# Routed expert tiles on one core: the down product moved ahead of the up product in TensorE's order

## The chip, the core and the metric

The kernel runs on one core of a Trainium2 chip. TensorE (PE in the views) multiplies matrices, VectorE (DVE), ScalarE (ACT) and GpSimd (POOL) work on elements, and SyncE (SP) issues DMAs. Each engine takes its own instructions in the order in which the program lists them, and they meet at semaphores. Matmuls read on-chip memory and write PSUM, which has 8 banks here, `ps[:, bank, :]`. The metric is device time in microseconds (us), lower is better.

## What is computed

Six sublayers on x of 8 sequences of 512 tokens with 256 features. Two of the six, the first and the third, are a mixture of experts, and the change lies in them:

```python
def _L0_ffn_ref(x, w12, w3, shared_w1, shared_w2, shared_w3, router_w, expert_bias):
    ...
    shared = silu(xf @ shared_w1.T) * (xf @ shared_w2.T) @ shared_w3.T
    scores = sigmoid(xf @ router_w.T)
    _, top_idx = top_k(scores + expert_bias, 2)
    gates = scores * one_hot(top_idx, 8).sum(axis=-2)
    h1, h2 = split(einsum('td,ehd->teh', xf, w12), 2)
    h = silu(h1) * h2 * gates[:, :, None]          # 8 experts, 256 hidden
    return shared + einsum('teh,edh->td', h, w3)

x = x + 0.5 * _L0_ffn_ref(_layernorm(x), ...)      # sublayer 1: changed code
x = x + _L0_attn_ref(_layernorm(x), ...)           # gated linear attention
x = x + 0.5 * _L0_ffn_ref(_layernorm(x), ...)      # sublayer 3: changed code
x = x + 0.5 * _L1_ffn_ref(_layernorm(x), ...)      # ternary feed-forward
x = x + _L1_attn_ref(_layernorm(x), ...)           # windowed attention
x = x + 0.5 * _L1_ffn_ref(_layernorm(x), ...)
```

Each token uses 2 of 8 experts. A product keeps float32 accuracy by splitting both operands into two float16 halves, high and low, and adding three matmuls (`mm3`, lines 2035 to 2037: high x high, high x low, low x high).

## The kernel before

The function `ffn0(n)` runs for sublayers 0 and 2. While the shared experts of the 8 sequences are worked on, the rows of every token are scattered in DRAM into regions of their experts. They are then taken as **71 tiles** of 128 rows (`TILES`), each of one expert. The tiles run after the shared work of the seventh sequence; the shared work of the eighth follows them.

A tile passes through these steps, each with its line:

- SyncE loads its rows into `tile_x` (L640; 4 buffers), once the product of the tile four back is done (`tile_prod`).
- TensorE transposes them into bank 0 or 1 (L2232, two matmuls of 128x128 in float32).
- ScalarE copies the gate (L1030) and the high half of the turned rows (`t_hi`, L1031); VectorE takes a row number (L1690) and the low half (`t_lo`, L1691).
- VectorE copies the expert's up weights from `later` into one of two slots (L1678).
- **Up product**, TensorE: 24 matmuls of 128x128 (`ps<-work` at L2035 to L2037) into bank 2 or 3. It waits for the weights, `tile_hi`, `tile_lo` and for the product of two tiles back, which empties the bank.
- ScalarE takes silu of one half (L1045), VectorE multiplies with the other (L1703, `tile_prod`).
- ScalarE takes the high half of that product (`th_hi`, L1038), VectorE the low half (`th_lo`, L1696).
- **Down product**, TensorE: 6 matmuls with 256 columns (`ps<-later,work` at L2035 to L2037) into bank 6 or 7. It waits for `th_hi`, `th_lo` and for the y of two tiles back. Its weight columns are found with a register that `pe.load` filled three steps earlier.
- ScalarE scales by the gate (L1051, `tile_y`), GpSimd scatters the rows to DRAM (L796).

The tiles are software-pipelined. Step i on each engine handles several tiles at once; `has(k)` says whether tile i-k exists. The orders within step i are:

- PE: transposes of tile i, up product of tile i-1, register load for tile i, down product of tile i-3
- ACT: gate and `t_hi` of i, `th_hi` of i-2, silu of i-1, y of i-3
- DVE: weight copy of i, row number and `t_lo` of i, `th_lo` of i-2, product of i-1

Steps 0 and 1 stand inside the seventh sequence's work, 2 to 7 are written out, 8 to 67 are a loop on the engine with four steps in its body, and 68 to 73 are written out again, the last two inside the shared units of the eighth sequence. The order is written by hand; no scheduler changes it.

Of the kernel before, what the change touches and what calls it, by code (L numbers as in the profile page):

```python
# [20 lines left out]
D = 256  # L21
KT = D // P
NSEQ, SEQ = 8, 512
# [7 lines left out]
SU, EU = HSH // P, HE // P  # L31
# [71 lines left out]
def ds(at, n):  # L103
    return bass.ds(at, n)


def build(nc, T, out):

    ctx = ExitStack()
    with ctx:  # L110
# [32 lines left out]
        def later_at(name, rows=P):  # L143
            at = 0
            for n, w in LATER.items():
                if n == name:
                    return later[0][0:rows, at:at + w], later[1][0:rows, at:at + w]
                at += w

        wup, wdn = later_at("w_up"), later_at("w_dn")  # L150
# [56 lines left out]
        ps = ctx.enter_context(nc.psum_tensor("ps", [P, 8, 512], F32))  # L207
# [47 lines left out]
        def earlier(n):  # L255

            return SUBLAYERS[:n].count("ffn0")
# [59 lines left out]
        def ffn0_space():  # L317

            r, at = Carve(), Carve()
            m = Space()  # L320
            m.h_hi, m.h_lo = r([SU, SEQ], F16), r([SU, SEQ], F16)
            at.at = r.at
            m.t_hi, m.t_lo = at([2, KT, P], F16), at([2, KT, P], F16)
            m.t_silu, m.t_prod = at([2, HE]), at([2, HE])
            m.th_hi, m.th_lo = at([2, EU, P], F16), at([2, EU, P], F16)
            m.t_y = at([4, D])
            m.silu, m.prod = r([2, SEQ]), r([PRODS, SEQ])
            assert at.at <= r.at
            m.scores, m.biased, m.rank, m.row = (r([TPS, NE]) for _ in range(4))
            m.mask = r([TPS, NE], F16)  # L330
            slot = Carve()
            slot.at = r.at
            m.beats, m.ties = r([TPS, NE, NE]), r([TPS, NE, NE])
            m.more = r([NE, NSEQ * TPS])
            m.over = r([TILES, NE])
            slots = [slot([2, KT, 2 * HE], F16), Carve()([2, KT, 2 * HE], F16)]
            assert slot.at <= r.at
            m.slots = slots
            m.tile_gate = r([4])
            m.onehot, m.picked = r([TOPK, TPS * NE]), r([TOPK, TPS * NE])  # L340
            m.gate, m.scatter_rows = r([2, TOPK, TPS]), r([2, TOPK, TPS], I32)
            m.base = r([NE])
            m.count, m.tiles, m.end, m.jump = (r([NE]) for _ in range(4))
            m.tile_x, m.zeros = r([4, RW]), r([RW])
            m.homes = r([TILES], I32)
            m.xn = (xn, m.tile_x)
            m.sums = r([2, TILES])
            m.before = r([NE, NE])
            m.table = r([2 * TILES + NE], I32)
            return m  # L350
# [198 lines left out]
        def in_slot(v):  # L549

            return 16 * len(range(v, TILES, 4))
# [1480 lines left out]
        def _(pe):  # L2032
            def mm3(out_, a, b, start, stop):

                nc.tensor.matmul(out_, a[0], b[0], start=start, stop=False)  # L2035
                nc.tensor.matmul(out_, a[0], b[1], start=False, stop=False)  # L2036
                return nc.tensor.matmul(out_, a[1], b[0], start=False, stop=stop)  # L2037

            def both(w, sl):
                return w[0][:, sl], w[1][:, sl]  # L2040
# [66 lines left out]
            def ffn0(n):  # L2107
                s, m = S[n], ffn0_space()
                G0, T0 = earlier(n) * NSEQ, earlier(n) * TILES
# [24 lines left out]
                def body(g, u):  # L2134
# [29 lines left out]
                    for q in range(SU):  # L2164
                        if is_first(g) and not earlier(n) and q % 4 == 0:
                            pe.wait_ge(w_lo_done, 3 if q == 0 else 5)
                        if q or not unit_ahead(n, g):
                            up(q)
                        if is_second(g) and earlier(n) and q == 2:
                            pe.wait_ge(tern_used, TERN_PARTS)  # L2170
                            pe.wait_ge(s["y_taken"], (g + G0) * 2 + 2)
                            for part in range(TERN_PARTS // 2):
                                ins = nc.tensor.matmul(ps[:, 7, 0:2], const("ones"), tsum[:, part], start=part == 0,
                                                       stop=part == TERN_PARTS // 2 - 1)
                            ins.then_inc(tern_step, 1)
                        if is_first(g):
                            if q == 3:
                                positions(0)
                            if q == 5:
                                pe.wait_ge(s["rows_ready"], G0 + 2)  # L2180
                                transposes(N0(n) + 1, m.xn[1])
                        elif is_second(g):
                            if q == 1:
                                pe.wait_ge(s["rows_ready"], G0 + 3)
                                transposes(N0(n) + 2, m.xn[0])
                            if q == 3:
                                router(2, 0)
                        elif is_last(g):
                            if q < 2:
                                tile_at(step, TILES + 1 + q)  # L2190
                        elif q == (2 if second_last(g) else 3):
                            positions(g + 1)
# [32 lines left out]
                def columns(u, back):  # L2225
                    return pe.snap(own_columns[(u - back) % 4], min_val=0, max_val=(NE - 1) * 2 * HE)

                def step(i, b, u, has):
                    if has(0):
                        pe.wait_ge(s[f"tile_in{u}"], 16 * (b + 1) + in_slot(u) * earlier(n))  # L2230
                        for k in range(KT):
                            ins = nc.tensor.transpose(ps[:, u % 2, k * P:(k + 1) * P], m.tile_x[:, u, k * P:(k + 1) * P], ident)  # L2232
                        ins.then_inc(s["tile_turned"], 1)
                    if has(1):
                        j, v = i - 1, (u - 1) % 2
                        pe.wait_ge(s["tile_weights"], j + 1 + T0)
                        pe.wait_ge(s["tile_hi"], j + 1 + T0)
                        pe.wait_ge(s["tile_lo"], j + 1 + T0)
                        if not isinstance(j, int) or j >= 2:
                            pe.wait_ge(s["tile_prod"], j - 1 + T0)  # L2240
                        for part in range(4):
                            own = slice(part * P, (part + 1) * P)
                            for k in range(KT):
                                ins = mm3(ps[:, 2 + v, own], [m.slots[v][:, h, k, own] for h in range(2)],
                                          (m.t_hi[:, v, k], m.t_lo[:, v, k]), k == 0, k == KT - 1)
                        ins.then_inc(s["tile_up"], 1)
                    if has(0):
                        pe.load(own_columns[u], m.table[0:1, ds(TILES + i, 1)])
                    if has(2) and isinstance(i, int) and i > TILES:
                        pe.wait_ge(s["tile_prod"], i - 1 + T0)  # L2250
                    if has(3):
                        j, v = i - 3, (u - 3) % 2
                        at = columns(u, 3)
                        pe.wait_ge(s["th_hi"], j + 1 + T0)
                        pe.wait_ge(s["th_lo"], j + 1 + T0)
                        if not isinstance(j, int) or j >= 2:
                            pe.wait_ge(s["tile_y"], j - 1 + T0)
                        else:
                            pe.wait_ge(s["y_taken"], 2 * (NSEQ - 1 + G0) + 1 + j)
                        for k in range(EU):  # L2260
                            ins = mm3(ps[:, 6 + v, 0:D], (m.th_hi[:, v, k], m.th_lo[:, v, k]), both(wdn, ds(at + k * D, D)),
                                      k == 0, k == EU - 1)
                        ins.then_inc(s["tile_down"], 1)
                if not n:
                    opening_unit(n)
                router(0, 0)
# [521 lines left out]
```

## Time and profile before

| What | us |
|---|---|
| Median of 3 runs | 1613.22 |
| Lowest and highest | 1610.5 and 1614.11 |
| Profiled execution, its own time | 1622.21 |
| Its span from the first to the last instruction | 1620.3 |
| First pass of tiles, from the transposes of tile 4 to those of tile 70 | 151.09 |
| Second pass, the same | 151.49 |

Around the span lie 1.9 us of the execution's own time. TensorE's granted clock is 1.00, full speed, over the whole span. A busy share counts the time in which some instruction of the engine is under way; a matmul's record is longer than the distance to the next one's start, so starts are compared below, not durations. In the rows on work, `idle before` is idle time of that engine ahead of the instruction, and the name behind the arrow is what ended it.

### The profile page before, as it was taken

What the parts mean: (1) busy time and instruction counts of PE and PEld (TensorE: products, weight loads), DVE (VectorE), ACT (ScalarE), POOL (GpSimd) and SP (SyncE); (2) the same over time, 40 slices, a digit from 0 to 9 for tenths busy, and PEclk for the clock granted to TensorE, in tenths of its full rate; (3) what the DMA queues carried; (4) which work ended last, traced back from release to release, by engine and by line L of the source; (5) the groups of instructions that cost most, each with busy time, mean ns of one, the idle gap of its engine ahead of it and who ended that gap; (6) DMA issues with size and microseconds to landing.
All of it is one profiled execution on the core that took longest, in us unless ns stands there. A gap on an engine that the chain in (4) does not pass through costs nothing.

```text
span 1620.3 us, 47107 instructions
## 1 busy us (share of the span) xinstructions
PE 1576.9 (97%) x17302; PEld 1138.1 (70%) x17303; DVE 1209.1 (75%) x2545; ACT 958.2 (59%) x1812; POOL 759.3 (47%) x676
## 2 busy tenths in 40 slices
PE   7999999999999999999999999999999999998998
PEld 3665568999656776666555669998566777877576
DVE  7677776777666766768866568777788878888876
ACT  5354544666477767763433336666476676674764
POOL 2342242545246566543333324555245567767343
PEclk9999999999999999999999999999999999999999
DMA  7132233333311211003310123333432022221001
GB/s 267 53 104 90 89 101 90 112 116 117 94 31 27 39 26 26 1 1 102 95 37 33 36 80 105 114 117 102 101 67 50 2 83 73 67 62 42 27 26 53
DMA packets 91308, 115.81 MB, mean 71 GB/s; under 512 B 9424, under 2 KB 76528, under 8 KB 91184
## 3 DMA queue, kind: packets, MB, share of 16 engines
q1 hardware_dynamic: 70832, 71.21, 15.0%
q0 software_dynamic: 20352, 42.88, 9.3%
q8 instruction: 87, 1.43, 0.4%
q14 instruction: 37, 0.30, 0.1%
HBM read 66.14 MB, written 47.90 MB: 70 GB/s over the span
## 4 chain that ended last, share of the span: by engine, by line
PE 84%; DVE 6%; ACT 3%; issue 3%; POOL 2%; DMA 1%; SPq 1%; another core or an unknown queue 0%; DVEq 0%; ACTq 0%; POOLq 0%
PE ps L2035 20%; PE ps L2037 19%; PE ps L2036 19%; PE ps L2327 3%; PE ps L2328 3%; PE ps L2277 3%; PE ps L2278 3%; PE ps L2051 2%; PE ps L2232 2%; PE ps L2567 2%; PE ps L2601 2%; PE ps L2579 1%; PE ps L2429 1%; PE ps L2454 1%; PE ps L2389 1%
## 5 line engine op out<-in xcount | busy, mean ns | idle before, releaser
L796 POOL DMA_INDIRECT routed<-work x142 | 163.8, 1153 | 198.3 <-ACT work L1051 194.3
L2035 PE MATMUL ps<-work 128*128 128x128 f16 x1136 | 197.8, 219 | 2.9 <-DVE work L1678 1.4
L2037 PE MATMUL ps<-work 128*128 128x128 f16 x1136 | 197.6, 219 | 0.0
L2036 PE MATMUL ps<-work 128*128 128x128 f16 x1136 | 197.5, 219 | 0.0
L2035 PE MATMUL ps<-xt_hi,wsh 128*128 128x512 f16 x508 | 192.6, 379 | 3.7 <-DVE work L1565 3.0
L2037 PE MATMUL ps<-xt_hi,wsh 128*128 128x512 f16 x508 | 192.5, 379 | 0.0
L2036 PE MATMUL ps<-xt_lo,wsh 128*128 128x512 f16 x508 | 192.5, 379 | 0.0
L984 ACT ACTIVATE work<-ps 128x512 f32<-128x512 f32 x128 | 76.2, 597 | 166.1 <-PE ps L2037 154.6
L1565 DVE SCALAR_TENSOR_TENSOR work<-ps,work 128x512 f32<-128x512 f32 x128 | 88.1, 690 | 81.1 <-ACT work L984 71.1
L2035 PE MATMUL ps<-wsh,work 128*128 128x256 f16 x512 | 139.5, 273 | 0.7 <-DVE work L1494 0.6
L2037 PE MATMUL ps<-wsh,work 128*128 128x256 f16 x512 | 139.6, 273 | 0.1
L2036 PE MATMUL ps<-wsh,work 128*128 128x256 f16 x512 | 139.5, 273 | 0.0
L2035 PEld LDWEIGHTS ps<-work 128*128 128x128 f16 x1136 | 111.0, 98 | 11.7 <-issue 5.3
L1078 ACT ACTIVATE work<-ps,cols 128x512 f32<-128x512 f32 x120 | 82.8, 691 | 57.8 <-PE ps L2278 44.4
L2327 PE MATMUL ps<-w2q,work 128*128 128x256 f16 x512 | 113.4, 273 | 0.0
L2328 PE MATMUL ps<-w2q,work 128*128 128x256 f16 x512 | 113.4, 273 | 0.0
L2036 PEld LDWEIGHTS ps<-work 128*128 128x128 f16 x1136 | 111.1, 98 | 0.7
L2037 PEld LDWEIGHTS ps<-work 128*128 128x128 f16 x1136 | 111.1, 98 | 0.0
L1741 DVE TENSOR_TENSOR work<-work 128x512 f16<-128x512 f32 x128 | 98.4, 797 | 14.5 <-ACT work L1065 12.7
L949 ACT ACTIVATE xt_hi<-ps 128x1024 f16<-128x1024 f32 x49 | 50.1, 1023 | 93.5 <-PE ps L2051 59.5
L2277 PE MATMUL ps<-xt_hi,w1q 128*128 128x512 f16 x256 | 97.1, 379 | 5.1 <-DVE xt_lo L1385 3.1
L1678 DVE COPY work<-later 128x2048 f16 x142 | 97.3, 685 | 5.2 <-PE ps L2037 3.8
(279 smaller groups left out, 4699.1 us busy)
## 6 DMA issues: line engine op xcount, KB each, us to landing
work<-expert_x SPq DMA_DIRECT2D x142, 129.0 KB
later<-values SPq DMA_DIRECT2D x32, 256.0 KB, 3.5
yg<-in_w_later SPq DMA_DIRECT2D x9, 498.0 KB
w1q<-in_w_later SPq DMA_DIRECT2D x9, 498.0 KB
yg<-in_w SPq DMA_DIRECT2D x16, 256.0 KB
values<-wsh SPq DMA_DIRECT2D x8, 512.0 KB, 4.3
out_x<-x SPq DMA_DIRECT2D x8, 512.0 KB, 2.9
expert_x<-work SPq DMA_DIRECT2D x30, 129.0 KB
```

The costliest lines, as they stand in the source:

```text
L796: nc.gpsimd.indirect_dma_start(routed[:, :], bass.IndirectOffsetOnAxis(m.homes[:, i:i + 1], 0), m.t_y[:, i % 4, :], None).then_inc(s[f"til ...
L984: nc.scalar.activation(m.silu[:, k % 2, :], ps[:, up_bank(g, k), :], ACT.Silu, scale=1 / WS).then_inc(s["silu_ready"], 1)
L1078: nc.scalar.activation(relu[:, k % RELUS, :], ps[:, 2 + k % 4, :], ACT.Relu, bias=b1_col[:, k:k + 1]).then_inc(s["relu_ready"], 1)
L1565: nc.vector.scalar_tensor_tensor(out=m.prod[:, k % PRODS, :], in0=ps[:, up_bank(g, k) + 1, :], scalar=HS / WS, in1=m.silu[:, k % 2, :], op ...
L1678: nc.vector.tensor_copy(m.slots[u % 2], up_of[:, :, :, ds(at, 2 * HE)]).then_inc(s["tile_weights"], 1)
L1741: nc.vector.tensor_tensor(h_lo[:, u, k, :], relu[:, k % RELUS, :], h_hi[:, u, k, :], ALU.subtract).then_inc(s["h_lo_ready"], 1)
L2035: nc.tensor.matmul(out_, a[0], b[0], start=start, stop=False)
L2036: nc.tensor.matmul(out_, a[0], b[1], start=False, stop=False)
L2037: return nc.tensor.matmul(out_, a[1], b[0], start=False, stop=stop)
L2277: nc.tensor.matmul(ps[:, 2 + q % 4, :], w, xt_hi[:, u, k, TOK], start=(k == 0), stop=False)
L2327: nc.tensor.matmul(o, h_hi[:, u, q, sl], w, start=(q == 0), stop=False)
L2328: ins = nc.tensor.matmul(o, h_lo[:, u, q, sl], w, start=False, stop=(q == FU - 1))
```

## The change

One block of `step` on TensorE is moved, without a change within it: the down product of tile i-3 stands right behind the transposes of tile i and ahead of the up product of tile i-1. The register load and the extra wait of the last steps stay behind the up product. The other engines' programs are the same.

```diff
@@ -2231,6 +2231,19 @@
                             ins = nc.tensor.transpose(ps[:, u % 2, k * P:(k + 1) * P], m.tile_x[:, u, k * P:(k + 1) * P], ident)
                         ins.then_inc(s["tile_turned"], 1)
+                    if has(3):
+                        j, v = i - 3, (u - 3) % 2
+                        at = columns(u, 3)
+                        pe.wait_ge(s["th_hi"], j + 1 + T0)
+                        pe.wait_ge(s["th_lo"], j + 1 + T0)
+                        if not isinstance(j, int) or j >= 2:
+                            pe.wait_ge(s["tile_y"], j - 1 + T0)
+                        else:
+                            pe.wait_ge(s["y_taken"], 2 * (NSEQ - 1 + G0) + 1 + j)
+                        for k in range(EU):
+                            ins = mm3(ps[:, 6 + v, 0:D], (m.th_hi[:, v, k], m.th_lo[:, v, k]), both(wdn, ds(at + k * D, D)),
+                                      k == 0, k == EU - 1)
+                        ins.then_inc(s["tile_down"], 1)
                     if has(1):
                         j, v = i - 1, (u - 1) % 2
                         pe.wait_ge(s["tile_weights"], j + 1 + T0)
@@ -2248,19 +2261,6 @@
                         pe.load(own_columns[u], m.table[0:1, ds(TILES + i, 1)])
                     if has(2) and isinstance(i, int) and i > TILES:
                         pe.wait_ge(s["tile_prod"], i - 1 + T0)
-                    if has(3):
...
```

TensorE before, in a step that is written out: behind the up product, the down product and then the next step's transposes (`TENSOR_LOAD` is the register load, `ISA` register arithmetic, `later` the down weights, and the names in brackets are the semaphores waited for).

```order
L2248 TENSOR_LOAD work
L2035 ISA [waits ffn00_tile_y,ffn00_th_lo,ffn00_th_hi]
L2035 MATMUL ps<-later,work 128x256
L2036 ISA
L2036 MATMUL ps<-later,work 128x256
L2037 MATMUL ps<-later,work 128x256
L2035 ISA
L2035 MATMUL ps<-later,work 128x256
L2036 ISA
L2036 MATMUL ps<-later,work 128x256
L2037 MATMUL ps<-later,work 128x256
L2232 MATMUL ps<-consts,work 128x128 [waits ffn00_tile_in2]
```

The wait for `th_hi` and `th_lo` stands there behind 24 up matmuls. TensorE now, at the same step: the down product between the transposes and the first up matmul.

```order
L2232 MATMUL ps<-consts,work 128x128
L2035 ISA [waits ffn00_tile_y,ffn00_th_lo,ffn00_th_hi]
L2035 MATMUL ps<-later,work 128x256
L2036 ISA
L2036 MATMUL ps<-later,work 128x256
L2037 MATMUL ps<-later,work 128x256
L2035 ISA
L2035 MATMUL ps<-later,work 128x256
L2036 ISA
L2036 MATMUL ps<-later,work 128x256
L2037 MATMUL ps<-later,work 128x256
L2035 MATMUL ps<-work 128x128 [waits ffn00_tile_lo,ffn00_tile_prod,ffn00_tile_hi,ffn00_tile_weights]
```

The whole up product now stands behind the wait for `th_hi` and `th_lo`. In the first steps of the loop's body the value to wait for is itself worked out in registers. TensorE there, before:

```order
L2248 ISA
L2248 TENSOR_LOAD work
L2257 REGISTER_ALU [waits ffn00_th_lo,ffn00_th_hi]
L2035 ISA [waits ffn00_tile_y]
L2035 MATMUL ps<-later,work 128x256
```

And now:

```order
L2261 TENSOR_LOAD work
L2232 MATMUL ps<-consts,work 128x128 [waits ffn00_tile_in1]
L2232 MATMUL ps<-consts,work 128x128
L2226 ISA
L2240 REGISTER_ALU [waits ffn00_th_lo,ffn00_th_hi]
L2035 ISA [waits ffn00_tile_y]
L2035 MATMUL ps<-later,work 128x256
```

The up product's last matmul is followed by the load and the next transposes, and the arithmetic moved with the down product.

## Rows read from the trace of the kernel before

**Rows 1.** The page: busy time by engine, and the last-ending chain by engine.

```profile
PE 1576.9 (97%) x17302; PEld 1138.1 (70%) x17303; DVE 1209.1 (75%) x2545; ACT 958.2 (59%) x1812; POOL 759.3 (47%) x676
...
PE 84%; DVE 6%; ACT 3%; issue 3%; POOL 2%; DMA 1%; SPq 1%; another core or an unknown queue 0%; DVEq 0%; ACTq 0%; POOLq 0%
```

**Rows 2.** Busy us (instructions) per engine, clock, DMA: stretch, its length, values.

```profile
249.00:265.00 16.00, 14.24 (x189) 12.91 (x190) 10.76 (x30) 7.31 (x24) 1.92 (x2) 1.00 0.27 75
...
259.67:410.76 151.09, 150.93 (x2114) 139.58 (x2113) 119.93 (x330) 103.05 (x329) 76.25 (x66) 1.00 0.37 114
975.86:1127.35 151.49, 151.24 (x2115) 139.44 (x2113) 119.78 (x330) 102.67 (x330) 77.37 (x66) 1.00 0.38 114
```

**Rows 3.** Timeline of PE (start, duration, line, work): transposes of tiles 4 and 70.

```profile
259.67 0.38 PE L2232 MATMUL ps<-consts,work 128*128 128x128 f32 x2
...
410.76 0.38 PE L2232 MATMUL ps<-consts,work 128*128 128x128 f32 x2
```

**Rows 4.** Timeline of PE over one step: up, down, transposes, up.

```profile
302.35 0.22 PE L2037 MATMUL ps<-work 128*128 128x128 f16 x1
302.41 0.27 PE L2035 MATMUL ps<-later,work 128*128 x1
...
303.06 0.38 PE L2232 MATMUL ps<-consts,work 128*128 128x128 f32 x2
303.28 0.22 PE L2035 MATMUL ps<-work 128*128 128x128 f16 x1
...
304.56 0.22 PE L2037 MATMUL ps<-work 128*128 128x128 f16 x1
```

**Rows 5.** Timeline of DVE behind a silu: product, weight copy, `t_lo`, `th_lo`.

```profile
301.34 0.42 DVE L1703 SCALAR_TENSOR_TENSOR work<-ps,work 128x256 f32<-128x256 f32 x1 [0.48 <-ACT work L1045]
301.69 0.68 DVE L1678 COPY work<-later 128x2048 f16 x1
...
302.53 0.42 DVE L1691 TENSOR_TENSOR work<-ps,work 128x256 f16<-128x256 f32 x1
302.86 0.42 DVE L1696 TENSOR_TENSOR work<-work 128x256 f16<-128x256 f32 x1
```

**Rows 6.** Timeline of ACT in the same step: silu, y, `t_hi`, `th_hi`, next silu.

```profile
300.93 0.38 ACT L1045 ACTIVATE work<-ps 128x256 f32<-128x256 f32 x1 [0.76 <-PE ps L2037]
301.21 0.47 ACT L1051 ACTIVATE work<-ps,work 128x256 f32<-128x256 f32 x1
...
301.90 0.36 ACT L1031 ACTIVATE work<-ps 128x256 f16<-128x256 f32 x1
302.17 0.41 ACT L1038 ACTIVATE work<-work 128x256 f16<-128x256 f32 x1
303.31 0.38 ACT L1045 ACTIVATE work<-ps 128x256 f32<-128x256 f32 x1 [0.74 <-PE ps L2037]
```

**Rows 7.** Timelines of PE, DVE and ACT near the start of the first pass.

```profile
256.94 0.22 PE L2037 MATMUL ps<-work 128*128 128x128 f16 x1
...
257.01 0.42 DVE L1691 TENSOR_TENSOR work<-ps,work 128x256 f16<-128x256 f32 x1
...
257.20 0.39 ACT L1045 ACTIVATE work<-ps 128x256 f32<-128x256 f32 x1 [1.42 <-PE ps L2037]
...
257.34 0.42 DVE L1696 TENSOR_TENSOR work<-work 128x256 f16<-128x256 f32 x1
...
257.68 0.22 PE L2035 MATMUL ps<-work 128*128 128x128 f16 x1 [0.30 <-DVE work L1691]
```

**Rows 8.** Waits in the first pass: who waited for whom, us, times, longest.

```profile
ACT work L1045 <- PE ps L2037: 27.8, 43, 0.9
```

**Rows 9.** Timeline of PE: last up matmul and first down matmul of a step.

```profile
391.61 0.22 PE L2037 MATMUL ps<-work 128*128 128x128 f16 x1
391.83 0.28 PE L2035 MATMUL ps<-later,work 128*128 x1
```

More of the change, by code:

```diff
@@ L2250, in step @@
                         pe.wait_ge(s["tile_prod"], i - 1 + T0)
-                    if has(3):
[L2252 to L2263, printed above, removed]
                 if not n:
```

## The prediction

> **What bounds the kernel now.** I read the page first: TensorE is busy 97% of the span and is 84% of the chain that ended last [rows 1]. The change touches only the routed tiles, so the next view was the busy time of the two stretches in which the loop over tiles runs. There PE is busy all the time by the modelled ends of its matmuls (150.93 of 151.09 us, 151.24 of 151.49 us) [rows 2]. Busy says little here, since each matmul overlaps the next; what counts is the start of one step's transposes to the next. Tile 4's transposes start at 259.67 and tile 70's at 410.76, which is 66 steps in 151.09 us or 2.289 us a step [rows 3]; the second pass has 66 steps in 151.49 us, 2.295 us [rows 2]. The mean is 2.292.
>
> What would a step be without any wait? Transposes take 0.22 (303.06 to 303.28), the 24 matmuls of the up product 1.34 (303.28 to the last start at 304.56 and one more of 0.056), the 6 of the down product 0.65 (302.41 to 303.06): 2.21 us [rows 4]. So TensorE loses only 0.08 us a step, 134 x 0.08 = 10 us in both passes. That is all a new order can win.
>
> **The change part by part.** The order of instructions differs on PE alone; ScalarE, VectorE, GpSimd and SyncE keep theirs. No instruction is added or removed, and no DMA is moved. Step i ran: transposes of tile i, up product of tile i-1, down product of tile i-3. Now the down product stands in the middle. Two things follow.
>
> First, the down product loses the cover of the up product. It waits for both halves of the activated hidden rows (`th_hi`, `th_lo`). Behind it on PE now stands the whole up product, which waits for nothing that comes that late; and behind that, ScalarE and VectorE.
>
> Second, the up product ends 0.65 us later in its step, directly ahead of the next step's transposes. All work on its result starts 0.65 us later.
>
> So I follow one tile j from the end of its up product to its down product. It is now: up product of j in step j+1, then transposes, down(j-1), up(j+1) in step j+2, transposes, down(j) in step j+3. The tile's own path is this:
>
> - Last up matmul starts, silu starts: 0.26 us (256.94 to 257.20) [rows 7]. It can be 0.96 (302.35 to 303.31) [rows 4, 6]; more on that below.
> - Silu start 300.93; product on VectorE 301.34; next tile's weight copy 301.69; the next tile's low half 302.53; this tile's `th_lo` 302.86, ended 303.28 [rows 5, 6]. ScalarE meanwhile does y 301.21, the next tile's high half 301.90 and this tile's `th_hi` at 302.17 [rows 6], in time. Silu start to the end of `th_lo`: 2.35 us. I checked which links really touch: the VectorE starts follow each other at 0.34 to 0.84 us with no idle printed, so neither the earlier y nor an earlier transpose shortens this; VectorE's queue is in program order and holds the copy and the next tile's low half ahead of `th_lo`.
> - `th_lo` ended, PE starts: the nearest row is PE's wait for a low half, ended at 257.01 + 0.42 = 257.43, first up matmul 257.68: 0.25 us [rows 7].
> - The down product needs register arithmetic for its weight columns ahead of its first matmul. Where PE's issue is barely ahead, that shows: 391.61 to 391.83 is 0.22 us between starts that are 0.06 apart elsewhere [rows 9]. After a real wait nothing is issued ahead, so I add 0.10. The bounds are 0 and 0.16 and I take a value inside, since part of it overlaps the wake-up.
>
> From the last up matmul of j to the first down matmul of j: 0.26 + 2.35 + 0.25 + 0.10 = 2.96 us. From there to the last matmul of up(j+2), which stands right behind: 0.65 + 1.28 = 1.93 us [rows 4]. Sum 4.89 us, and it closes a loop that covers **two** steps: 2.45 us a step. Its floor with no arithmetic at all is 4.79 / 2 = 2.40. PE's own 2.21 lies below, so the bound moves from PE's throughput to this loop. In the kernel before, the same path had the up product's 1.34 us more to be done in, and cost nothing.
>
> The stalls that exist today (0.08 us a step, mostly the up product waiting for a low half) lie inside the new wait: the up product now comes 0.65 us later in its step, so its operands are ready.
>
> Sum: 2.45 - 2.292 = 0.158 us, times 67 steps (66 and one at the end where down(68) meets the same path) = 10.6 us a pass. At the start down(0) follows tile 3's transposes: `th_lo` ends at 257.34 + 0.42 = 257.76, plus 0.25 + 0.10 gives 258.11, then 0.65 of down; up(2) starts at 258.76 and its step ends at 260.10, where tile 4's transposes started at 259.67 [rows 3, 7]: 0.4 us. A pass loses 11.0 us, both 22 us. Nothing behind hides it: the last sequence's shared units follow on PE, and that is the chain. The remaining cover changes little: SyncE's tile loads are issued off the product of four tiles back, and loop and load stretch together.
>
> The profiled execution took 1622.2 us, 9 above the median of 1613.2; the stretches above are 19% of it, so I apply the 22 us to the median unchanged: **1635 us**, 1.4% slower.
>
> **The rivals.**
>
> *Late release of the up product's result (slower still).* In the loop, silu follows the last up matmul by 0.26 us in some steps and by 0.96 in others [rows 4, 6, 7]; ScalarE's wait for it is 27.8 us in 43 steps of the first pass, 0.65 each [rows 8]. Today that is harmless. If it stays in half of the steps, the loop of two steps grows by 0.5 x 0.70 = 0.35 us, 0.175 a step: 134 x 0.175 = 23 us more, **1658 us**. For it: half of the steps have it, and I found no waited-for event that explains it. Against it: where PE's issue stands at a wait when the up product ends, as at 256.94, the release is prompt, and the new order puts such a wait into each step.
>
> *Next to nothing happens.* If PE resolves the wait and the arithmetic while `th_lo` is finishing (no 0.25, no 0.10), the loop is 4.54 / 2 = 2.27 us, a hair under today's 2.292: **1611 to 1616 us**. Against it: each measured wait of PE on VectorE costs 0.25. It would also be the outcome if the new wait merely replaced the old one.
>
> *Faster.* The up product no longer waits for the low half, whose place is 0.65 us later. If `th_lo` also came in time, the 0.08 us a step would go: 134 x 0.08 = 10 us, **1603 us**. The point that decides is whether the path of a tile fits into 4.43 us (two steps of 2.21). By the rows it takes at least 4.79, so VectorE's copy or its order would have to be faster than it is.
>
> *The clock falls.* PE now rests about 0.24 us a step. The granted clock was 1.00 in the stretch at the start of the pass too, where PE was busy 14.24 of 16 us, 89% [rows 2], the same share as 2.21 / 2.45 = 90%. If it fell to 1.2 GHz, 134 steps of 2.21 us would double: some 300 us. I give it 1 in 100. The Trainium skill ("TensorE: Matmul & The Clock Gate", Part 1) says that the clock is gated down when the engine is idle and speaks of K as binary, so a fall would be to half and plain in the trace. By that page too 300 us would be the price; that the row with 89% busy kept 1.00 speaks against it here.
>
> **How the numbers follow.** 1635 and its neighbourhood (1624 to 1648) 0.58; late release (1648 to 1670) 0.20; next to nothing 0.13; faster 0.08; clock 0.01. The bounds of the one unknown cost (2.40 to 2.48 a step) make 1629 to 1639 alone. Leaving out the faster case, half of the second and the far end of the late one gives 1614 to 1658. A difference of under 0.2% (3 us) can't be told from no change on this kernel: faster 0.08, within 0.10, slower 0.82.
>
> **What would show it right or wrong.** Right: a new wait of PE (or its weight load) in front of the `later` matmuls, put down to VectorE's `th_lo` (L1696), some 130 times at 0.2 to 0.5 us; PE's step at 2.40 to 2.5 us; the last up matmul followed directly by the transposes; VectorE's order unchanged with `th_lo` ending about 2.6 us after the last up matmul; the low half's wait ahead of the up product gone; the rest of the span unchanged. Wrong: steps of 2.2 to 2.3 us (PE's wait is cheaper than I measure), or steps of 2.6 with silu starting 0.9 us after the last up matmul (late release), or most of the loss outside of the two tile stretches.

## The result, and the profile after

The changed kernel takes 1640.9 us (median of 4 runs, 1640.4 to 1642.0), the kernel before in the same comparison 1613.4 us (4 runs). The ratio is 1.0177, with a 95% interval of 1.0163 to 1.019: 27.5 us slower, 1.8%. The forecast was 1635.

The page of the changed kernel, busy time by engine and the chain, which answer to [rows 1]:

```profile
PE 1593.7 (97%) x17302; PEld 1125.6 (69%) x17303; DVE 1213.6 (74%) x2545; ACT 953.3 (58%) x1812; POOL 777.2 (47%) x676
...
PE 83%; DVE 6%; issue 3%; ACT 3%; POOL 2%; DMA 1%; SPq 0%; DVEq 0%; ACTq 0%; POOLq 0%
```

These lines say next to nothing: the same instructions, and TensorE at 97% as before. The loss is in the stretches of the tiles. Windows of the changed kernel from the transposes of tile 4 to those of tile 70, both passes, with the columns of [rows 2]:

```profile
259.52:420.95 161.43, 158.24 (x2116) 133.55 (x2113) 122.92 (x330) 100.83 (x330) 85.18 (x66) 1.00 0.36 106
986.31:1147.93 161.62, 159.07 (x2115) 133.16 (x2113) 122.69 (x330) 100.79 (x330) 85.23 (x66) 1.00 0.35 106
```

66 steps take 161.43 and 161.62 us, 2.446 and 2.449 us a step; they took 2.289 and 2.295 [rows 2, 3]. The clock is still 1.00. PE's busy time is 98% of the stretch even now. The second column, the weight loads, tells more: 133.55 of 161.43 us is 83%, and it was 139.58 of 151.09, 92% [rows 2]. The Trainium skill ("Perfetto Trace Analysis", Identifying the Most-Contended Engine) says that busy time of matmuls is a poor measure of headroom, since they are pipelined, and to judge by the share of peak arithmetic or of the weight loads instead; this trace agrees in direction. The size is less exact: part of the fall from 92% to 83% is that as many weight loads are busy for 133.55 us instead of 139.58.

Waits of the changed kernel in the first of these stretches (who waited for whom, us, times, longest):

```profile
ACT work L1045 <- PE ps L2037: 54.9, 66, 1.6
DVE work L1703 <- ACT work L1045: 35.3, 66, 1.2
PEld ps L2035 <- issue: 15.3, 55, 0.4
```

The third line is the new wait. It is not put down to `th_lo` (L1696), as I had said it would be, but to "issue": what waits is a register instruction ahead of the first down matmul, and that one has no record of work. So it must be read from the starts. The timeline of PE in the changed kernel, one step and the start of the next (start, duration, line, work):

```profile
320.19 0.22 PE L2037 MATMUL ps<-work 128*128 128x128 f16 x1
320.24 0.39 PE L2232 MATMUL ps<-consts,work 128*128 128x128 f32 x2
320.75 0.28 PE L2035 MATMUL ps<-later,work 128*128 x1
...
321.32 0.27 PE L2037 MATMUL ps<-later,work 128*128 x1
321.45 0.21 PE L2035 MATMUL ps<-work 128*128 128x128 f16 x1
...
322.74 0.22 PE L2037 MATMUL ps<-work 128*128 128x128 f16 x1
322.79 0.39 PE L2232 MATMUL ps<-consts,work 128*128 128x128 f32 x2
323.07 0.28 PE L2035 MATMUL ps<-later,work 128*128 x1
```

The transposes need 0.22 us, but the down product starts 0.51 and 0.28 us behind them. VectorE in the same stretch:

```profile
319.97 0.41 DVE L1696 TENSOR_TENSOR work<-work 128x256 f16<-128x256 f32 x1
321.02 0.42 DVE L1703 SCALAR_TENSOR_TENSOR work<-ps,work 128x256 f32<-128x256 f32 x1 [0.64 <-ACT work L1045]
321.37 0.68 DVE L1678 COPY work<-later 128x2048 f16 x1
322.04 0.16 DVE L1690 TENSOR_TENSOR work<-work,consts 128x1 f32 x1
322.12 0.42 DVE L1691 TENSOR_TENSOR work<-ps,work 128x256 f16<-128x256 f32 x1
322.45 0.41 DVE L1696 TENSOR_TENSOR work<-work 128x256 f16<-128x256 f32 x1
```

`th_lo` ends at 319.97 + 0.41 = 320.38, and the down matmul follows at 320.75; it ends at 322.86, and the next follows at 323.07. And ScalarE:

```profile
320.52 0.38 ACT L1045 ACTIVATE work<-ps 128x256 f32<-128x256 f32 x1 [0.99 <-PE ps L2037]
320.80 0.47 ACT L1051 ACTIVATE work<-ps,work 128x256 f32<-128x256 f32 x1
321.38 0.20 ACT L1030 ACTIVATE work<-work 128x1 f32<-128x1 f32 x1
321.49 0.37 ACT L1031 ACTIVATE work<-ps 128x256 f16<-128x256 f32 x1
```

The last up matmul starts at 320.19, silu at 320.52, `th_lo` of that tile ends at 322.86, its down product starts at 323.07. I took the four parts of this path over the steps of both passes (tiles 4 to 67, 64 in each), from the records:

| Part of the path | forecast | measured, mean (range) |
|---|---|---|
| last up matmul to silu | 0.26 | 0.275 (0.25 to 0.34) |
| silu to the end of `th_lo` | 2.35 | 2.35 (2.19 to 2.51) |
| end of `th_lo` to first down matmul | 0.25 + 0.10 | 0.278 (0.20 to 0.54) |
| first down matmul to last up matmul | 1.93 | 2.00 (1.94 to 2.11) |
| sum, over two steps | 4.89 | 4.90 |

4.89 / 2 = 2.45 is the step that was forecast, 2.447 the one that is there. The sum alone proves nothing: the four parts lead from the up product of tile j to that of tile j+2, so they add up to two steps whatever binds. What speaks for the loop is that each part has about its forecast length, and that PE's wait behind `th_lo` is at its shortest, 0.20 to 0.22 us, in half of the steps. In the other half it is 0.34 us or more; nearly all of those are the first two steps of the loop's body, where the value to wait for is worked out in registers. What was mis-sized is the other end of the subtraction, the step of the kernel before.

### The profile page after: what moved, and what is told of

It is laid out like the page before. It is cut to its first block, busy times and chain, and to the rows that moved or that the text cites. A ratio compares the mean times of both kernels' runs of the same rounds, so it can differ in the third digit from the quotient of the medians.

```text
span 1640.1 us, 47092 instructions
## 1 busy us (share of the span) xinstructions
PE 1593.7 (97%) x17302; PEld 1125.6 (69%) x17303; DVE 1213.6 (74%) x2545; ACT 953.3 (58%) x1812; POOL 777.2 (47%) x676
## 4 chain that ended last, share of the span: by engine, by line
PE 83%; DVE 6%; issue 3%; ACT 3%; POOL 2%; DMA 1%; SPq 0%; DVEq 0%; ACTq 0%; POOLq 0%
PE ps L2035 20%; PE ps L2036 19%; PE ps L2037 18%; PE ps L2328 3%; PE ps L2327 3%; PE ps L2277 3%; PE ps L2278 3%; PE ps L2051 2%; PE ps L2232 2%; PE ps L2567 2%; PE ps L2601 2%; PE ps L2579 1%; PE ps L2429 1%; POOL expert_x L768 1%; PE ps L2454 1%
## 5 line engine op out<-in xcount | busy, mean ns | idle before, releaser
L796 POOL DMA_INDIRECT routed<-work x142 | 180.7, 1273 | 203.3 <-ACT work L1051 199.1
L1045 ACT ACTIVATE work<-ps 128x256 f32<-128x256 f32 x142 | 54.4, 383 | 121.1 <-PE ps L2037 121.1
L1703 DVE SCALAR_TENSOR_TENSOR work<-ps,work 128x256 f32<-128x256 f32 x142 | 60.2, 424 | 78.3 <-ACT work L1045 78.3
```

The costliest lines, as they stand in the source:

```text
L796: nc.gpsimd.indirect_dma_start(routed[:, :], bass.IndirectOffsetOnAxis(m.homes[:, i:i + 1], 0), m.t_y[:, i % 4, :], None).then_inc(s[f"til ...
L1045: nc.scalar.activation(m.t_silu[:, v], ps[:, 2 + v, 0:HE], ACT.Silu, scale=1 / WS).then_inc(s["tile_silu"], 1)
L1703: nc.vector.scalar_tensor_tensor(out=m.t_prod[:, v], in0=ps[:, 2 + v, HE:2 * HE], scalar=HS / WS, in1=m.t_silu[:, v], op0=ALU.mult, op1=AL ...
```

## Experiments

Each was timed beside runs of the kernel before on the same chip, whose medians were 1612.8, 1612.4 and 1612.9 us. Times are medians; ratios are against those runs.

### The kernel before, once more

No edit. The profiled execution of [rows 2] was 9 us above the median, and I had called that spread over the kernel. Where does a usual execution differ?

> The kernel before, unchanged, to see why its profiled execution took 1622.2 us when the others take 1613. Theory A (the excess lies in the tile steps, whose length varies from execution to execution because the up product's result is seen late in some of them): other steps than before see it late, the two tile passes differ from 151.1 and 151.5 us by a few us, the rest of the span by under 1 us. Theory B (the excess lies elsewhere, or is the profiler's): the passes are within 0.5 us of 151.1 and 151.5 again. Time beside the kernel before: no difference, ratio 1.000 within 0.002.

Measured: 1613.8 us (11 runs), ratio 1.0004 (0.9995 to 1.0013). Windows of this second execution of the kernel before, transposes of tile 4 to those of tile 70:

```profile
258.03:406.13 148.10, 148.07 (x2114) 140.39 (x2113) 119.39 (x331) 108.19 (x330) 63.80 (x66) 1.00 0.38 116
969.10:1117.39 148.29, 148.26 (x2114) 140.25 (x2113) 119.22 (x331) 108.17 (x330) 63.92 (x66) 1.00 0.39 116
```

2.244 and 2.247 us a step, mean 2.245, not 2.289 and 2.295. The waits in its first stretch, of which the last line answers to [rows 8]:

```profile
DVE work L1690 <- ACT work L1031: 24.6, 65, 0.5
...
ACT work L1045 <- PE ps L2037: 12.7, 50, 0.5
```

Silu waits for the up product 12.7 us here and 27.8 us in [rows 8], and it follows the last up matmul by 0.27 us on average (0.25 to 0.34), where it was 0.63 (0.26 to 1.06) in the first execution. So the late release belongs to that one execution; none of the traces of the other kernels has it either. The two executions differ by 10.9 us in span (1620.3 and 1609.4). 3.0 + 3.2 = 6.2 us of that lie in these two stretches, and 4.7 us outside of them, where Theory A had allowed under 1: it holds for the stretches alone. The typical step of the kernel before is 2.245 us, 0.04 above PE's own 2.21, and that is no wait for the low half: `t_lo` ended 0.39 us or more before the up product in every step. Of the four steps of the loop's body two take 2.21, one 2.25 and the one that starts behind the loop's branch 2.32 on average. Its transposes are followed by the up product after 0.32 instead of 0.22:

```profile
302.70 0.43 PE L2232 MATMUL ps<-consts,work 128*128 128x128 f32 x2
305.02 0.38 PE L2232 MATMUL ps<-consts,work 128*128 128x128 f32 x2
307.23 0.38 PE L2232 MATMUL ps<-consts,work 128*128 128x128 f32 x2
```

### The down product one and two quarters into the up product

If the loop over two steps sets the time, cover brings it back by known amounts. The up product consists of four parts; one, or two of them, go ahead of the down product again:

```diff
+                    def down_product():
+                        if not has(3):
+                            return
...
                     if has(1):
...
                         for part in range(4):
+                            if part == 1:                # and part == 2
+                                down_product()
```

One quarter:

> The down product stands behind the first of the four parts (6 of 24 matmuls, 0.33 us) of the up product. My theory (a loop over two steps: last up matmul of tile j, silu, product, weight copy, low halves, down(j), the rest of up(j+2)): the first part no longer counts in the loop, 4.89 - 0.33 = 4.56 us, 2.28 us a step, some 0.17 us under the change: about 1619 us, 22 us faster than the change and 6 slower than before. Rival (the loss is the exposed wake-up and register arithmetic ahead of the down matmuls, 0.2 us a step wherever the block stands): 1638 to 1642.

Measured: 1619.8 us, ratio 1.0042 (1.0027 to 1.0058); steps of 2.289 and 2.288 us. Two quarters:

> The down product stands behind half of the up product. My theory: the loop is 4.89 - 0.67 = 4.22 us, below two steps of 2.21 us of TensorE's own work, so the loop no longer binds and the time is that of the kernel before: 1609 to 1616 us. Rival (exposed wake-up wherever it stands): about 1640. Any value clearly under 1610 would say that the down product's place also costs something in the kernel before.

Measured: 1613.8 us, ratio 1.0006 (0.9997 to 1.0015); steps of 2.253 and 2.25 us. The path up to the end of `th_lo` keeps its length in both (0.275 + 2.36). What changes is what follows: with two quarters the down product starts 0.60 us after `th_lo` ended, so it no longer waits for it; with one quarter 0.33. 0.33 us of cover give back 21 us of the 28, the next 0.33 the remaining 6. Against the kernel before there is nothing to win, as [rows 4] had said: PE's own work is the floor.

The kernel with one quarter was run a second time, once; in spite of the label, the edit of the activated rows is not in it:

> Withdrawn in favour of a kernel of its own under another label; one look at the down product behind one of four parts again: 1619 to 1620 us, steps of 2.29 us.

It took 1620.3 us, with steps of 2.293 and 2.29 us, and says no more than the first.

### The down product ahead of the transposes

The opposite: one step earlier still.

```diff
+                    if has(3):
+                        ...                              # the down product's block, unchanged
                     if has(0):
                         pe.wait_ge(s[f"tile_in{u}"], 16 * (b + 1) + in_slot(u) * earlier(n))
```

> One place further: the down product of tile i-3 also stands ahead of the transposes of tile i. By the two-step loop alone, the transposes' 0.22 us come into it: 5.11 us, 2.56 us a step, 1656 us. But now the transposes wait for th_lo too, and t_hi on ScalarE, which th_hi and th_lo are queued behind, waits for the transposes: a loop of one step, t_hi start to th_lo end 1.37, to the down product 0.35, down product 0.65, transposes to t_hi 0.45, sum 2.82 us. My theory takes the longer: 2.8 us a step, 0.37 x 134 = 50 us over the change, 1680 to 1695 us. Rival (the loss of the change is a fixed exposed wake-up per step, wherever the block stands): 1640.

Measured: 1700.5 us, ratio 1.0546 (1.0528 to 1.0563); steps of 2.877 and 2.881 us. VectorE and ScalarE of this kernel:

```profile
320.95 0.16 DVE L1690 TENSOR_TENSOR work<-work,consts 128x1 f32 x1 [0.79 <-ACT work L1031]
```

```profile
320.30 0.20 ACT L1030 ACTIVATE work<-work 128x1 f32<-128x1 f32 x1 [0.92 <-PE ps L2245]
```

PE's transposes are at L2245 here. Now ScalarE waits for the transposes, VectorE for ScalarE, `th_lo` stands behind that, the down product waits for `th_lo`, and the next transposes stand behind the down product: a loop that closes in one step, as expected. The time missed the expected range by 5.5 us. Over both passes the parts are 1.37 (start of `t_hi` to the end of `th_lo`), 0.27, 0.69 and 0.56, together 2.89 us, where 1.37, 0.35, 0.65 and 0.45 had been expected: the way from the transposes to `t_hi` was taken 0.11 too short.

### The activated rows ahead of the next tile's halves

In the changed kernel, `th_hi` and `th_lo` of tile i-2 go ahead of `t_hi` and `t_lo` of tile i, on ScalarE and on VectorE:

```diff
+                    if has(2):
+                        ...                              # th_hi (VectorE: th_lo), unchanged
                     if has(0):
                         ...                              # gate, t_hi (VectorE: row number, t_lo)
-                    if has(2):
-                        ...
```

> The change, and on ScalarE and VectorE the halves of the activated rows (th_hi, th_lo of tile i-2) are taken ahead of the halves of the turned rows (gate, t_hi, row number, t_lo of tile i). My theory: th_lo leaves two VectorE instructions behind it, 0.41 us, so the loop is 4.48 us, 2.24 us a step: 0.21 x 134 = 28 us back, 1613 us. The up product has 0.65 us of room for the later t_lo. Rival (the loss is in TensorE's issue, the wait on th_lo only shows it): at least 1635. Rival (the later t_lo becomes the bound of the up product): 1620 to 1635, with PE's wait put down to L1691.

Measured: 1616.6 us, ratio 1.0025 (1.0015 to 1.0034); steps of 2.275 and 2.277 us. Silu to the end of `th_lo` shrinks from 2.35 to 1.83 us, and the change costs 4 us instead of 28. So the path through `th_lo` is shown as the cause from its other side: the order on TensorE is that of the change, and only its predecessors are earlier. The expected 2.24 was not reached. PE's starts show three steps of 2.22 us and one of 2.41 to 2.47 in turn; PE of this kernel:

```profile
301.11 0.39 PE L2232 MATMUL ps<-consts,work 128*128 128x128 f32 x2
301.33 0.27 PE L2035 MATMUL ps<-later,work 128*128 x1
...
303.33 0.39 PE L2232 MATMUL ps<-consts,work 128*128 128x128 f32 x2
303.72 0.28 PE L2035 MATMUL ps<-later,work 128*128 x1
```

In three steps the down product follows the transposes at once (0.22), in the fourth after 0.39. In that fourth step the trace has, among the instructions of PE that do no work, the register load of the step before (302.45, 0.30 long), the loop's branch (302.90, 0.21 long), and then five more of 0.04 to 0.05 each, about 0.1 apart, the last at 303.61 right ahead of the matmul. One of the five is a wait, and it takes no longer than the others, since `th_lo` ended at 303.08 (302.66 + 0.42 on VectorE). PE's own program is late, once in the four steps of the loop's body, by about 0.2 us.

The same edit in the kernel before:

> The kernel before with th_hi, th_lo ahead of t_hi, t_lo: control for the two runs with that order. The path through t_lo becomes 0.26 + 2.35 + 0.25 + 1.28 = 4.14 us for two steps, still under 4.43, so 1610 to 1616 us, the same as before. Rival (t_lo comes too late for the up product, which has no down product ahead of it here): up to 0.1 us a step, 1620 to 1627 us.

Measured: 1612.9 us, ratio 1.0003 (0.9994 to 1.0013), steps of 2.24 and 2.248 us. There the path has slack, and shortening it buys nothing.

### Half of the weight copy

My prediction had named VectorE's queue alone as the chain: product, weight copy, low half, `th_lo`. Then a copy of half the size must give its time back. Only the high half of the weights is copied (128x1024 instead of 128x2048), and the up product uses it in place of the low half as well, with the same number of matmuls:

```diff
-                    nc.vector.tensor_copy(m.slots[u % 2], up_of[:, :, :, ds(at, 2 * HE)]).then_inc(s["tile_weights"], 1)
+                    nc.vector.tensor_copy(m.slots[u % 2][:, 0:1], up_of[:, 0:1, :, ds(at, 2 * HE)]).then_inc(s["tile_weights"], 1)
...
-                                ins = mm3(ps[:, 2 + v, own], [m.slots[v][:, h, k, own] for h in range(2)],
+                                ins = mm3(ps[:, 2 + v, own], [m.slots[v][:, 0, k, own] for h in range(2)],
```

In the changed kernel:

> The change, but VectorE copies only the high half of the up weights (128x1024 instead of 128x2048) and the up product uses it in place of the low half too, so the result differs; TensorE's work is the same. The copy stands between the product and th_lo. My theory (two-step loop through VectorE): the copy gives back 0.34 us, of which 0.20 to 0.25 counts, because th_hi on ScalarE ends 1.64 us after silu's start and th_lo can't start ahead of 1.72 instead of 1.93. Loop 4.67 us, 2.34 us a step, 0.11 x 134 = 14 us under the change: 1624 to 1628 us. Rival (TensorE's issue after the move): no effect, 1640.

Measured: 1640.8 us, ratio 1.0176 (1.0159 to 1.0193), steps of 2.443 and 2.449 us. No effect at all; the expectation failed. VectorE of this kernel:

```profile
319.70 0.42 DVE L1703 SCALAR_TENSOR_TENSOR work<-ps,work 128x256 f32<-128x256 f32 x1 [0.63 <-ACT work L1045]
320.05 0.42 DVE L1678 COPY work<-later 128x1024 f16 x1
320.72 0.16 DVE L1690 TENSOR_TENSOR work<-work,consts 128x1 f32 x1 [0.26 <-ACT work L1031]
```

The copy takes 0.42 instead of 0.68, and VectorE then idles 0.26 for ScalarE's `t_hi`. `t_hi` starts 0.97 us after silu and ends 0.37 later, both here (319.20, 320.17) and in the changed kernel (320.52, 321.49). L1690 follows 0.18 after that end in both. Over all 128 steps of the changed kernel, L1690 starts within 0.19 us of `t_hi`'s end in 97 and never more than 0.08 us after the end of the copy. So two chains of nearly equal length lead from silu to L1690: on VectorE product and copy, on ScalarE y, gate and `t_hi`. Idle time of zero in front of VectorE's instruction had not told that ScalarE was just as late.

The kernel before with half of the copy:

> The same halved weight copy in the kernel before (result differs in the same way). My theory: there the path of a tile has the up product's 1.34 us as slack, the loop does not bind, and the copy is free: 1610 to 1614 us, within 3 us of before. If VectorE were near the bound there too, it would gain 5 us or more.

Measured: 1610.6 us, ratio 0.9989 (0.9979 to 0.9998), steps of 2.243 us in both passes, as expected: the steps are those of the kernel before (2.245) within 0.003 us.

### y behind silu, alone and with half of the copy

If two chains tie, cutting one gives nothing and cutting both gives the time. ScalarE's chain is cut by taking y(i-3) ahead of silu(i-1) instead of behind it:

```diff
+                    if has(3):
+                        ...                              # y, unchanged
                     if has(1):
                         ...                              # silu
-                    if has(3):
-                        ...
```

Alone:

> The change, and ScalarE takes y of tile i-3 ahead of silu of tile i-1 (the down product is now done early in the step, and ScalarE was idle ahead of silu). Theory after the halved weights (two chains of equal length lead from silu to the low halves: on VectorE product and weight copy, on ScalarE y and t_hi; cutting one alone gives nothing): no effect, since the weight copy on VectorE still ends where it did, 1636 to 1642 us, step 2.43 to 2.45. Rival (ScalarE's chain alone binds, the copy had room): y's 0.59 us leave the loop, up to 0.2 a step, 1613 to 1625 us.

Measured: 1643.3 us, ratio 1.0189 (1.0172 to 1.0206), steps of 2.459 and 2.458 us: nothing gained, as expected, though the time lies 1 us above the expected range. `t_hi` now ends 0.59 us or more ahead of L1690, which still follows the end of the copy within 0.02 us in 95 of 128 steps. With half of the copy:

> Both cuts together: y ahead of silu, and VectorE copies only the high half of the up weights, which the up product uses for both (result differs). By the theory of two equal chains the low halves now start about 0.4 us earlier behind silu: loop 4.89 - 0.42 = 4.47 us, 2.24 us a step, 27 us under the change: 1611 to 1617 us. By the rival that only one of the chains binds, it equals whichever single cut worked; if neither did (1640), the loop does not run through them at all.

Measured: 1635.2 us, ratio 1.0136 (1.0119 to 1.0153), steps of 2.426 and 2.427 us. Both together gain what neither gains alone, but 6 us and not the 27 expected. Of the 6, only 2.7 us lie in the two stretches of 66 steps; the rest lies outside of them, where two executions of the kernel before differ by as much. That the two chains tie rests on the records above, then, more than on this gain. VectorE of this kernel in an early and in a late step (silu is at L1052 here):

```profile
320.94 0.43 DVE L1703 SCALAR_TENSOR_TENSOR work<-ps,work 128x256 f32<-128x256 f32 x1 [0.90 <-ACT work L1052]
321.28 0.42 DVE L1678 COPY work<-later 128x1024 f16 x1
321.80 0.16 DVE L1690 TENSOR_TENSOR work<-work,consts 128x1 f32 x1
...
325.51 0.42 DVE L1703 SCALAR_TENSOR_TENSOR work<-ps,work 128x256 f32<-128x256 f32 x1 [0.71 <-ACT work L1052]
325.98 0.43 DVE L1678 COPY work<-later 128x1024 f16 x1
326.88 0.16 DVE L1690 TENSOR_TENSOR work<-work,consts 128x1 f32 x1 [0.47 <-issue]
```

In the first step L1690 comes 0.86 after the product, in the other 1.37, with 0.47 us of idle time put down to issue: no engine is waited for, VectorE's own program is late. Its records between the product and L1690 are, in the late step, the loop's branch (325.60), register arithmetic, and a register load (L1687) at 326.11 that takes 0.49 us; in the early step there is no branch, and the load stands at 321.19 and takes 0.35. "Issue" ahead of L1690 is 8.6 us in 24 of 59 steps in the stretch from 262 to 405 us; in the change it is hidden behind the copy. In this kernel silu to the end of `th_lo` is 2.10 us in the median, but up to 2.69 and 2.24 on average, only 0.11 under the 2.35 of the change. PE's first down matmul comes 0.39 us after `th_lo` on average, 0.11 later than in the change. The late register loads on VectorE are seen in the records; how much of the missing 0.19 us a step is theirs and how much PE's own program was not tried.

### One quarter of cover and the activated rows first

Each of these two alone had given most of the loss back, so both together should give all of it:

> Down product behind one of four parts of the up product, and th_hi, th_lo ahead of t_hi, t_lo. The loop with th first is 4.55 us (step 2.276 measured), less 0.33 is 4.22 us, below TensorE's own two steps of 4.43: the loop binds no more, and the time is that of the kernel before, 1610 to 1615 us, step 2.22 to 2.26. If the place of the down product cost anything beside the loop, it would stay over 1617.

Measured: 1640.4 us, ratio 1.0174 (1.0157 to 1.0191), steps of 2.452 and 2.446 us, by turns 2.62 to 2.71 and 2.22 to 2.33. As slow as the change: a miss by 27 us. PE of this kernel, from the transposes to the down product:

```profile
321.70 0.39 PE L2232 MATMUL ps<-consts,work 128*128 128x128 f32 x2
322.33 0.22 PE L2035 MATMUL ps<-work 128*128 128x128 f16 x1 [0.23 <-DVE work L1696]
...
322.66 0.27 PE L2035 MATMUL ps<-later,work 128*128 x1
```

VectorE of this kernel, where L1696 is `t_lo`:

```profile
321.66 0.42 DVE L1696 TENSOR_TENSOR work<-ps,work 128x256 f16<-128x256 f32 x1
```

The first quarter of the up product stands right behind the transposes and needs `t_lo`, which the swap has made the last on VectorE. It ends at 322.08, silu + 2.43 (319.65), and PE resumes at 322.33. From there: a quarter and the down product to the next up matmul (322.33 to 323.32, 0.99), three quarters (to the last start at 324.27, 0.95), 0.26 to silu: 2.43 + 0.25 + 0.99 + 0.95 + 0.26 = 4.88, again over two steps, 2.44. I had costed the path through `th_lo` and forgotten that the same edit lengthens the one through `t_lo`, and that the down product now lies inside it. With the down product first (1616.6 us above) it serves as the cover of `t_lo`.

## Why the prediction was right

**The mechanism.** A loop over two steps from the up product over silu, `th_lo` and the down product, forecast at 4.89 us, and two steps measured at 4.89. That this loop sets the step is shown by the runs that move it: cover of 0.33 and 0.67 us (2.288 and 2.25 a step) and a shorter way to `th_lo` (2.276); the place ahead of the transposes closes another loop, over one step (2.88). The 2.35 for silu to the end of `th_lo` came from a single step of an execution in which that stretch ranged from 2.19 to 3.04 and was 2.58 on average; in the second execution it never was under 2.57. It was the right row because it is one in which VectorE idles nowhere between; an average would have given 0.2 us too much.

**The floor.** 2.21 us of PE's own work, so that at most 10 us could be won. In the typical execution it is 0.035 x 134 = 5 us, and not, as I wrote, "mostly the up product waiting for a low half": the low half is in time there in every step. Right: no order tried was faster than the kernel before beyond the measurement. "Faster" (1603) failed at its condition, as the path takes 4.9 us and had to fit into 4.43.

**The mis-sized term.** 2.45 - 2.292 = 0.158 us a step. The 2.45 was right within 0.003, but 2.292 came from an execution 9 us above the median. I read that as a general excess. The second execution, 10.9 us shorter in span, shows that 6.2 of those lay in the very stretches from which I took the step. With 2.245 the term is 0.20 x 134 = 27 us, beside 27.5 measured. The step that failed is the sentence "so I apply the 22 us to the median unchanged": the 9 us should have been placed, or a doubt about 2.292 kept in the sum.

**The wake-up.** 0.25 + 0.10 forecast, 0.278 on average. The sum of 0.35 was right for one half of the steps (0.34 and more, as the 0.37 after 320.38) and 0.15 too much for the other (0.20 to 0.22). The down product with what stands behind it took 2.00 instead of 1.93. That the two errors cancel is luck.

**The start of the pass.** 0.4 us a pass was forecast. Against the second execution of the kernel before, 26.7 us of the 30.7 us in span lie in the two stretches of 66 steps and 4.0 us elsewhere, where two executions of the kernel before differ by more than that, so the span can't tell it. The step of tile 3 can, from its transposes to those of tile 4: 2.98 and 2.99 us in the two passes of the change, 2.67 to 2.68 in both executions of the kernel before. The start costs 0.3 us a pass.

**Late release.** It did not happen: silu follows by 0.25 to 0.34 us in every step. My reason was that PE stands at a wait, but the kernel before is as prompt in its second execution without one. What made the first execution late stays open. The rival deserved less than 0.20, since its row [rows 8] came from the same odd execution.

**Next to nothing.** Its condition, a wait that is resolved for free, did not hold: 0.20 us is the least seen. **The clock** stayed at 1.00 with the weight loads at 83%.

**Who holds VectorE.** "Neither the earlier y nor an earlier transpose shortens this" was right for y alone (1643.3 us), but the reason was incomplete. ScalarE's chain over y, gate and `t_hi` ends with VectorE's over the copy. The sum did not depend on it, but every plan to repair the change would have.

**Where it shows.** I expected some 130 waits put down to L1696. There were 55 in the first pass and 62 in the second, put down to issue ahead of a weight load; what waits there is an instruction that handles registers and has no record of work.

## What to carry to other kernels

In a loop that is pipelined over several engines, close each loop of dependences by hand, divide its length by the number of steps that it spans, and compare with the busiest engine's own work per step; moving a block takes cover from one wait and adds its length to every path that now runs through it. Before a difference of a few hundredths of a microsecond a step is multiplied by 134, see whether the profiled execution is a typical one. And an instruction that shows no idle time may still have a second predecessor that ends at the same moment: cut both before you count on the gain.

## What the runs showed of the hardware that I had not expected

- The same program had silu 0.63 us after the last up matmul on average in one execution and 0.27 in another; the step was 2.292 and 2.245 us. No cause was found.
- A copy of half the size on VectorE takes 0.42 instead of 0.68 us (128x1024 and 128x2048, two bytes an element).
- After a wait for VectorE, PE's first matmul starts 0.20 to 0.22 us after the end of the record in half of the steps, and 0.34 to 0.45 us in those in which the value to wait for is worked out in registers.
- Instructions without work count once the cover is gone: register loads of 0.30 to 0.49 us each in the steps shown, and a loop's branch of 0.21 us on PE. Up to 0.5 us of VectorE's idle time ahead of L1690 is of this kind in one kernel, and PE's step behind the branch is 0.2 us longer than the others in another. In the kernel before it is 0.1 us longer.
